# Expert choice: the second layer with its weights standing, the output tile turned back by two transposes

## What is computed

```python
E, S, D, M = (48, 4, 256, 256)
K = D // S                                    # 64
logits = xf @ Wr.T                            # 4096 x 48
vals, idx = jax.lax.top_k(logits.T, cap)      # cap = 128 tokens for each expert
w = jax.nn.softmax(vals, axis=-1)
xg = xf[idx]                                  # 48 x 128 x 256
h = jax.nn.gelu(jnp.einsum('ecd,esdm->ecsm', xg, W1) + b1[:, None], approximate=False)
y = jnp.einsum('ecsm,esmk->ecsk', h, W2) + b2[:, None]
y = y.reshape(E, cap, D) * w[..., None]
out = jnp.zeros_like(xf).at[idx.reshape(-1)].add(y.reshape(-1, D))
```

## Time and profile before

| | |
|---|---|
| time before, median of three runs | 4528.04 us (4521.71 to 4534.21) |
| time of the profiled execution | 4522.78 us |
| its span, first to last instruction | 4520.9 us |
| PE busy | 3809.7 us, 84% of the span |
| DVE busy | 2532.4 us, 56% |
| POOL busy | 2013.8 us, 45% |
| ACT busy | 1895.9 us, 42% |
| mean granted clock of PE | 0.930 |

### The profile page before, as it was taken

The page is one execution under the profiler, slowest core; times in us unless marked ns, Lnnn a source line. Parts: engine busy times, 40 slices in busy tenths (PEclk is TensorE's granted clock), DMA queues, the critical chain, the costliest instruction groups (busy, mean ns, idle before and its releaser), DMA issues. The chain is left out here.

```text
span 4520.9 us, 70654 instructions
## 1 busy us (share of the span) xinstructions
PE 3809.7 (84%) x26056; PEld 2647.9 (59%) x26088; DVE 2532.4 (56%) x4540; ACT 1895.9 (42%) x3440; POOL 2013.8 (45%) x2061
## 2 busy tenths in 40 slices
PE   7677787799999439948998799788888888999995
PEld 3546664467676239924554455466666666656663
DVE  6667453455554662247777322598888887412223
ACT  4132133333333102226666322588888886112222
POOL 6312462222223126632332111399999998332223
PEclk9788898899999769978999899899999999999997
DMA  5747541200000629945554200111111111822224
GB/s 192 242 144 218 150 117 64 75 10 10 13 17 8 222 74 296 288 122 150 150 145 135 84 29 28 51 52 50 52 50 44 49 45 58 273 89 46 46 45 133
DMA packets 334072, 459.67 MB, mean 102 GB/s; under 512 B 71222, under 2 KB 245750, under 8 KB 329606
## 3 DMA queue, kind: packets, MB, share of 16 engines
q1 hardware_dynamic: 311094, 424.27, 30.7%
q0 software_dynamic: 22512, 30.36, 3.6%
q10 hardware_dynamic: 128, 0.52, 0.0%
HBM read 314.54 MB, written 140.51 MB: 101 GB/s over the span
## 5 line engine op out<-in xcount | busy, mean ns | idle before, releaser
L3565 POOL TENSOR_TENSOR mamba_hC<-mamba_h_t,mamba_cb 128x512 f32<-128x512 f32 x512 | 677.7, 1351 | 70.4 <-DVE mamba_h_t L3078 64.5
L3078 DVE TENSOR_TENSOR_SCAN mamba_h_t<-mamba_dA,mamba_pB 128x512 f32<-128x512 f32 x512 | 596.8, 1206 | 122.1 <-PE mamba_pB L3456 46.0
L3456 PE MATMUL mamba_pB<-ident,mamba_dBT 128*128 128x128 f32 x2048 | 328.6, 285 | 55.4 <-DVE mamba_h_t L3078 49.5
L3254 ACT ACTIVATE mamba_dA<-mamba_delta,mamba_a_neg 128x512 f32<-128x512 f32 x512 | 356.7, 713 | 23.5 <-DVE mamba_h_t L3078 22.9
L3456 PEld LDWEIGHTS mamba_pB<-ident,mamba_dBT 128*128 128x128 f32 x2048 | 239.8, 144 | 191.9 <-issue 100.2
L3465 PE MATMUL mamba_pY<-ident,mamba_hC 128*128 128x128 f32 x2048 | 320.3, 280 | 15.8 <-POOL mamba_hC L3565 14.2
L1911 POOL TENSOR_SCALAR mqa_prob<-mqa_prob,mqa_rinv 128x128 f32<-128x128 f32 (+3 forms) x256 | 136.2, 532 | 425.4 <-DVE mqa_rinv L1687 424.4
L2350 DVE TENSOR_REDUCE mha_nmax<-mha_pM 128x1 f32<-128x384 f32 (+3 forms) x352 | 215.5, 634 | 104.0 <-PE mha_pM L2658 100.8
L3245 ACT ACTIVATE mamba_dBT<-mamba_eT,mamba_b_t 128x512 f32<-128x512 f32 x384 | 273.7, 713 | 0.1
L1501 POOL DMA_INDIRECT top_sum<-top_y,top_xg x71 | 110.3, 1554 | 352.1 <-ACT top_y L1290 341.5
L3465 PEld LDWEIGHTS mamba_pY<-ident,mamba_hC 128*128 128x128 f32 x2048 | 247.3, 145 | 25.2 <-POOL mamba_hC L3565 24.4
(11 more groups left out here) (618 smaller groups left out, 8877.8 us busy)
## 6 DMA issues: line engine op xcount, KB each, us to landing
expert_w<-in_L_ffn_W SPq DMA_DIRECT2D x48, 1024.0 KB, 5.9
delta_shared<-delta_w SPq DMA_DIRECT2D x64, 576.0 KB, 4.9
mamba_cb<-mamba_c SPq DMA_DIRECT2D x128, 256.0 KB, 3.2
mha_qkT<-mha_parts_d SPq DMA_DIRECT2D x96, 256.0 KB, 4.9
expert_w<-in_L_ffn_W SPq DMA_DIRECT2D x48, 256.0 KB, 6.4
top_w<-in_L_ffn_w SPq DMA_DIRECT2D x24, 512.0 KB, 10.6
delta_w<-delta_wst SPq DMA_DIRECT2D x17, 576.0 KB, 3.4
top_slots<-top_y SPq DMA_DIRECT2D x1, 9159.0 KB, 36.9
```

Source lines behind the costliest of these rows:

```text
L3078: nc.vector.tensor_tensor_scan(h_t[:, n % RH, :], dA[:, n % RA, :], pB[n % 2][:, :], 0.0, ALU.mult, ALU.add).then_inc(z["scan_ready"], 1)
L3254: nc.scalar.activation(dA[:, n % RA, :], delta[:, a % 2, ct, :], ACT.Exp, scale=a_neg[:, ct, s:s + 1])\
L3456: last = nc.tensor.transpose(pB[n % 2][:, tok(t)], dBT[:, r % RS, t, ct * P:(ct + 1) * P], c.ident[:, :])
L3565: nc.gpsimd.tensor_tensor(hC[:, n % RO, :], h_t[:, n % RH, :], cb[:, r % RC, :], ALU.mult)\
```

## The change

W2 becomes the standing operand: 128 x 64, and the hidden tile moves, 128 columns. The result has channels on partitions (64 of them for each part s), so two parts share a 128-partition tile `out_T`, one in its lower and one in its upper half; the products alternate between the halves. DVE adds b2 there as one number per partition (`add_b2`), PE turns the 128 x 256 tile back by two transposes (`turn_back`), and DVE only multiplies by the weight (`weigh`). b2 is loaded once for all experts, turned by two transposes beside those of b1, and no longer loaded and weighted for each expert. The order on PE is now `turn(e + 1)`, `hidden(e)`, `turn_back(e - 2)`, `output(e - 1)`, on DVE `add_b1(e)`, `weigh(e - 2)`, `add_b2(e - 1)`. The load of an expert waits for `yT_ps` of expert e - 5.

```diff
@@ -3678,23 +3678,26 @@
         b1T = sc.sb("b1T", [P, E * S, MT])
         w1 = sc.sb("w1", [P, WR, S, 2, M])
         w2 = sc.sb("w2", [P, WR, S, 2, K])
-        b2 = sc.sb("b2", [P, WR, D])
+        b2r = sc.sb("b2r", [E, D])
+        b2T = sc.sb("b2T", [P, E, 2])
         xg = sc.sb("xg", [P, GR, D])
         xgT = sc.sb("xgT", [P, 2, KD, P])
         hT = sc.sb("hT", [P, 2, S * MT, P])
+        yT = sc.sb("yT", [P, 2, 2, P])
         y = sc.sb("y", [P, YR, D])
         bank = [sc.ps(f"bank{k}", [P, L]) for k in range(4)]
         pH = [sc.ps(f"pH{k}", [P, S * MT, P]) for k in range(2)]
...
                  "rev_ps", "picked", "top_ps", "max_ready", "exp_ready", "wgt_done", "wgt_ps", "wgt_ready", "idx_ready",
-                 "x_ps", "x_ready", "h_ps", "hb_ready", "h_ready", "y_ps", "b2_ready", "y_ready", "dch", "pch")
+                 "x_ps", "x_ready", "h_ps", "hb_ready", "h_ready", "yT_ps", "yT_ready", "y_ps", "y_ready", "dch", "pch")
         z = {name: sc.sem(name) for name in NAMES}
         ring = lambda name, n: [sc.sem(f"{name}{i}") for i in range(n)]
         x_in, w_in = (ring(s, n) for s, n in (("x_in", XR), ("w_in", WR)))
         got, added = c.gathered, c.added
-        assert len(got) == GR
-        w_loads = 3 * 16
+        assert len(got) == GR and 2 * K == P and S == 4
+        w_loads = 2 * 16
+        out_T = [bank[2 + k][:, D:2 * D].rearrange("p (j t) -> p j t", j=2) for k in range(2)]
         pL = [pH[k][:, 0:S, :].rearrange("p s m -> p (s m)") for k in range(2)]
 
         with nc.Block() as block:
@@ -3703,13 +3706,11 @@
                 def load_expert(e):
                     r = e % WR
                     if e >= WR:
-                        sp.wait_ge(z["y_ready"], e - WR + 1)
+                        sp.wait_ge(z["yT_ps"], e - WR + 1)
                     sp.dma_start(w1[:, r, :, :, :].rearrange("p s k m -> p s (k m)"),
                                  w["L1_ffn_W1"][e].rearrange("s (p k) m -> p s (k m)", k=2)).then_inc(w_in[r], 16)
                     sp.dma_start(w2[:, r, :, :, :].rearrange("p s k m -> p s (k m)"),
                                  w["L1_ffn_W2"][e].rearrange("s (p k) m -> p s (k m)", k=2)).then_inc(w_in[r], 16)
-                    sp.dma_start(b2[:, r, :], w["L1_ffn_b2"][e:e + 1].rearrange("e s k -> e (s k)").to_broadcast([P, D]))\
-                        .then_inc(w_in[r], 16)
 
                 sp.dma_start(wr[:, :, :], w["L1_ffn_Wr"].rearrange("(k p) e -> p k e", p=P)).then_inc(z["wr_in"], 16)
                 for b in range(NB):
@@ -3725,7 +3726,8 @@
                     sp.dma_start(x[:, b % XR, :, :], rows(src)[b]).then_inc(x_in[b % XR], 16)
                     if b == 2:
                         sp.dma_start(b1r[:, :, :], w["L1_ffn_b1"].rearrange("(a e) s m -> (e s) a m", a=2))\
-                            .then_inc(z["b1_in"], 16)
+                            .then_inc(z["b_in"], 16)
+                        sp.dma_start(b2r[:, :], w["L1_ffn_b2"].rearrange("e s k -> e (s k)")).then_inc(z["b_in"], 16)
                     if b >= 2:
                         sp.wait_ge(z["xn_done"], b - 1)
                         if b == 2:
@@ -3784,10 +3786,12 @@
                         carry_stats(nc, dve, c, before, link)
                     if b == 3:
                         carry_scale(nc, dve, c, before)
-                dve.wait_ge(z["b1_ps"], 1)
+                dve.wait_ge(z["b_ps"], 1)
+                nc.vector.tensor_copy(b2T[:, :, :].rearrange("p e j -> p j e"),
+                                      bank[3][:, 2 * MT * ES:2 * MT * ES + 2 * E].rearrange("p (j e) -> p j e", j=2))
                 nc.vector.tensor_copy(b1T[:, :, :].rearrange("p (a e) k -> p a k e", a=2),
                                       bank[3][:, 0:2 * MT * ES].rearrange("p (a k e) -> p a k e", a=2, k=MT))\
-                    .then_inc(z["b1_ready"], 1)
+                    .then_inc(z["b_ready"], 1)
 
                 dve.wait_ge(z["lg_ready"], NB)
                 for i in range(CAP // 8):
@@ -3820,27 +3824,35 @@
                 def add_b1(e):
                     dve.wait_ge(z["h_ps"], e + 1)
                     if e >= 2:
-                        dve.wait_ge(z["y_ps"], e - 1)
+                        dve.wait_ge(z["yT_ps"], e - 1)
                     bias = b1T[:, e * S:(e + 1) * S, :].rearrange("p s k -> p (s k)")
                     nc.vector.tensor_tensor(hT[:, e % 2, :, :], pH[e % 2][:, :, :],
                                             bias.unsqueeze(2).to_broadcast([P, S * MT, P]), ALU.add)\
                         .then_inc(z["hb_ready"], 1)
 
+                def add_b2(e):
+                    dve.wait_ge(z["yT_ps"], e + 1)
+                    if e >= 2:
+                        dve.wait_ge(z["y_ps"], e - 1)
+                    nc.vector.tensor_tensor(yT[:, e % 2, :, :], out_T[e % 2], b2T[:, e, :].unsqueeze(2).to_broadcast([P, 2, P]),
+                                            ALU.add).then_inc(z["yT_ready"], 1)
+
                 def weigh(e):
                     dve.wait_ge(z["y_ps"], e + 1)
-                    dve.wait_ge(z["b2_ready"], e + 1)
                     if e >= YR:
                         dve.wait_ge(added[e % 2], 16 * ((e - YR) // 2 + 1))
-                    nc.vector.scalar_tensor_tensor(y[:, e % YR, :], bank[2 + e % 2][:, 0:D], wgtT[:, e:e + 1],
-                                                   b2[:, e % WR, :], ALU.mult, ALU.add).then_inc(z["y_ready"], 1)
-
-                dve.wait_ge(z["b1_ready"], 1)
+                    nc.vector.tensor_scalar(y[:, e % YR, :], bank[2 + e % 2][:, 0:D], wgtT[:, e:e + 1], None, ALU.mult)\
+                        .then_inc(z["y_ready"], 1)
+
+                dve.wait_ge(z["b_ready"], 1)
                 dve.wait_ge(z["wgt_ready"], 1)
-                for e in range(E + 1):
+                for e in range(E + 2):
                     if e < E:
                         add_b1(e)
-                    if e:
-                        weigh(e - 1)
+                    if e >= 2:
+                        weigh(e - 2)
+                    if 1 <= e <= E:
+                        add_b2(e - 1)
 
             @block.scalar
             def _(act):
@@ -3905,13 +3917,16 @@
                     if b:
                         scores(b - 1)
                 scores(NB - 1)
-                pe.wait_ge(z["b1_in"], 16)
+                pe.wait_ge(z["b_in"], 16 * 2)
                 pe.wait_ge(z["xT_ready"], NB)
                 for a in range(2):
                     for k in range(MT):
                         at = (a * MT + k) * ES
-                        last = nc.tensor.transpose(bank[3][:, at:at + ES], b1r[:, a, k::MT], c.ident[0:ES, 0:ES])
-                last.then_inc(z["b1_ps"], 1)
+                        nc.tensor.transpose(bank[3][:, at:at + ES], b1r[:, a, k::MT], c.ident[0:ES, 0:ES])
+                for j in range(2):
+                    at = 2 * MT * ES + j * E
+                    last = nc.tensor.transpose(bank[3][:, at:at + E], b2r[:, j * P:(j + 1) * P], c.ident[0:E, 0:E])
+                last.then_inc(z["b_ps"], 1)
 
                 pe.wait_ge(z["drawn"], 1)
                 for g, part in enumerate((first, second)):
@@ -3951,21 +3966,33 @@
                 def output(e):
                     pe.wait_ge(z["h_ready"], e + 1)
                     if e >= 2:
+                        pe.wait_ge(z["yT_ready"], e - 1)
+                    for j in range(2):
+                        for m in range(MT):
+                            for a in range(2):
+                                s = 2 * j + a
+                                last = nc.tensor.matmul(out_T[e % 2][K * a:K * (a + 1), j, :], w2[:, e % WR, s, m, :],
+                                                        hT[:, e % 2, s * MT + m, :], start=(m == 0), stop=(m == MT - 1),
+                                                        skip_group_check=True)
+                    last.then_inc(z["yT_ps"], 1)
+
+                def turn_back(e):
+                    pe.wait_ge(z["yT_ready"], e + 1)
+                    if e >= 2:
                         pe.wait_ge(z["y_ready"], e - 1)
-                    for s in range(S):
-                        for m in range(MT):
-                            last = nc.tensor.matmul(bank[2 + e % 2][:, s * K:(s + 1) * K], hT[:, e % 2, s * MT + m, :],
-                                                    w2[:, e % WR, s, m, :], start=(m == 0), stop=(m == MT - 1),
-                                                    skip_group_check=True)
+                    for j in range(2):
+                        last = nc.tensor.transpose(bank[2 + e % 2][:, j * P:(j + 1) * P], yT[:, e % 2, j, :], c.ident[:, :])
                     last.then_inc(z["y_ps"], 1)
 
                 turn(0)
-                for e in range(E + 1):
+                for e in range(E + 2):
                     if e + 1 < E:
                         turn(e + 1)
                     if e < E:
                         hidden(e)
-                    if e:
```

(17 more changed lines are left out.)

## The result

The changed kernel takes 4602.95 us (median of five, 4593.45 to 4605.19) against 4528.04: 1.0153 times the time before, with a 95% interval of 1.0135 to 1.0170. The forecast was 4510, the range 4500 to 4525.

The account below looks back on a forecast made before the run. PE was taken to bound the expert loop, transfers running as fast as it asks. Loop -18.2 plus 0.5 before it gave -17.7 us: 4505 profiled, 4510 for the median, which lies 5.2 above; range 4500 to 4525.

Parts of the forecast that it names:

- the sentence on POOL: POOL in the expert loop: scatter(e) one pass later, ring y four deep, costs zero but for the end.
- signs of being wrong: PE in the expert loop: waiting for `w_in` or `yT_ready` would show the forecast wrong; no size given.
- The clock: Rival, expert stage: clock at risk only if PE waited at a switch for DVE, with three us slack; no chance given.
- if the first layer's groups grow beyond 3.77: Sign of being wrong, PE's first layer: groups over 3.77 us would mean that transfers or loads meddle.
- The sum on PE: PE's sequence of one expert: 5.39 us instead of 5.77, a gain of 0.38.
- the forecast's 18.2: Loop over experts: gain of 17.5 us from 46 experts, plus 0.7 from the pass with the first output.
- switches of 0.1: PE changing array partition: 0.11 us on leaving the second layer, 0.09 on entering, 0.05 on the first transposes behind.
- Uncovered loads: Rival, second layer on PE: next weights' load not covered, expert 5.87 us, 4533; half uncovered 4522; chance 0.11.
- Transfers as the bound: Rival, loop's queues: no expert below 5.77 us once the cushion is used up, 7 us lost, 4517; chance 0.12.
- Serial halves: Rival, second layer on PE: halves don't run side by side, 1.74 us, expert 6.25, kernel 4550; chance 0.06.
- Before the loop: Ahead of the expert loop: two more transposes and one more copy cost 0.5 us, between 0.2 and 0.9.
- The end: From the last first layer to the last y: 5.1 us as before, so zero, give or take 0.3.

Follow-up runs that it names:

- cured kernel: Changed kernel with POOL doing scatter(e - 2) where it did scatter(e - 1), one pass more at the end: 4520.67 us, 0.9993 of before.
- the cure by a longer ring: Changed kernel with the ring of gathered rows five deep instead of four, scatter left in place: 4520.6 us, 0.9983 of before; again 4519.23 us, 0.9970.
- the lateness put alone into the kernel before: Kernel before with every gather issued one pass later, PE's work unchanged: 4638.3 us, 1.0265 of before.
- one half only: Cured kernel with the second-layer products of both parts written to the lower half of the partitions: 4567.49 us, 1.0066 of before.

## Why the prediction was wrong

- **The step that failed** is the sentence on POOL: "`scatter(e)` comes one pass later, with the ring y four deep; zero but for the end." It asked what the later scatter needs, not what stands behind it on its engine. Behind scatter(e - 1) stands gather(e + 4), and PE waits for that. The gather had 2.0 us of slack, as the POOL rows of before show, and the y ahead of it came 4.9 us later, 0.8 of them because `weigh` stands behind `add_b1` on DVE. PE waited 58.4 us for gathers in the loop. The waits that the forecast named as signs of being wrong were `w_in` and `yT_ready`, not this one. The cure by order alone, the cure by a longer ring, and the lateness put alone into the kernel before all show it.
- **The clock came with the waits.** The granted clock was 0.91 to 1.00 in stretches of 40 us, where it had been 1.00, and 15 us of the loop's loss are that. The forecast named the clock only for a wait on DVE. Its sign "if the first layer's groups grow beyond 3.77" came, but by the clock and not by transfers or loads.
- **The sum on PE was right.** 5.39 forecast, 5.45 measured in the cured kernel's passes (loop 15.0 us shorter; the forecast's 18.2 took 0.38 a pass for 0.33). The 0.06 are 0.02 in `turn`, 0.03 in the second layer, a few ns in the rest. Halves side by side, loads covered, switches of 0.1: as forecast, and with one half only the output group is 1.89, where the rival's sum had 1.74 + 0.11.
- **Uncovered loads**: refuted, as a round of two takes 0.11, the second layer 1.02 in all. The rival gave 5.87 or 5.63 a pass; the run gives 5.45. The Trainium skill (TensorE: Matmul & The Clock Gate, The mechanism) says that a load overlaps running products if the row group differs, or if it goes to the background buffer. Both halves use all rows here and their loads are covered, so this trace doesn't agree with the row group as the only condition.
- **Transfers as the bound**: refuted, 312 GB/s with no wait. But I used them only as a bound on rate; what counted was how long they made a gather take to land.
- **Serial halves**: refuted.
- **Before the loop** 0.5: from the first transposed bias to the first draw of tokens it is 1.64 us now (1533.30 to 1534.94) and was 1.24, so 0.4. Where the loop begins as a whole lies in the scatter of the profiles (1649.1 to 1660.6). **The end** 0: up to the last y it is 5.15 us (1991.11 to 1996.26), as forecast, but the stage's end cost 1.3 us in the changed kernel, since the last scatter had to wait 1.05 for the landing of the last but one on its sum.
- **The measure of the cured kernel**: 0.07 to 0.30% under before, 3 to 14 us, where 17.7 had been forecast. In the profiles the stage is 11 to 13 us shorter than before's 456 (445.1, 443.1 and 445.1 from its first transfer or transpose to the next stage's): 15 from the loop, less what beginning and end cost. The forecast took everything behind the stage as unchanged; the profiles don't bear that out, and why is open.

## What to carry to other kernels

When a result becomes ready a pass later, go to each instruction that waits for it and read on down that engine's queue: the next instruction there, which has nothing to do with the result, is late by a pass too. Its slack is in the trace, from issue to use less the landing, and it must be compared with how much later it starts. A queue with a wait in it wants the instructions that feed the bottleneck ahead of it, or one more place in their ring.

In these runs the landing of the small transfer was no property of its own: it changed with the large ones in the same queues. Read the two together.

## What the runs showed of the hardware

- The same gather of 128 rows landed in 2.8 us in queues without weights and in 5.4 to 6.8 with them (middle values of the changed kernel, 5.4, of before, 5.8, and of the cured ones, 6.7 and 6.8), and was used 8.1 us after its issue in a pass where it went out 0.6 us behind 1.25 MB.
- Products of 128 rows by 64 columns that go to different halves of the partitions overlap even when four instructions of one half follow each other: 1.08 us for 16 against 1.02 in turn and 1.89 in one half.
- The busy share of the DMA engines read 1.0 at 294 GB/s, and the same queues moved 312 GB/s without making PE wait.
- With PE waiting 1.3 us in a pass on the mean, stretches of 40 us had a mean granted clock of 0.91 to 1.00, where it was 1.00 without waits. With a wait of 2.6 to 3.9 us in every second pass the loop had 0.81.
